# Chunk-wise copies at the end of two expert stages, and layer 1's combine weights in exchanged PSUM banks

## The reference, cut to what matters

```python
# layer 0: 64 experts, 8 chosen for each token, and a shared one
routed = sum over e of combine[:, e, None] * (relu2(xf @ up_w[e]) @ down_w[e])
x = x + gb * (routed + relu2(xf @ shared_up_w) @ shared_down_w)
# layer 1: 8 experts, all of them for each token
g = x @ w_gate[e];  u = x @ w_up[e];  h = silu(g) * u
cw = router_probs * gate_weights;  cw = cw / (sum(cw) + 1e-9)
x = x + gb * sum over e of cw[:, e, None] * (h @ w_down[e])
```

## Time and profile before

| what | us |
|---|---|
| time, median of 3 runs | 1149.88 (1149.51 to 1150.43) |
| the profiled execution | 1148.7 |
| its span, first to last instruction | 1147.0 |
| PE busy | 1071.9 (93%) |
| DVE busy | 897.1 (78%) |
| ACT busy | 746.7 (65%) |
| POOL busy | 247.2 (22%) |
| mean granted clock of PE | 0.982 of full |

### The profile page before, as it was taken

How to read it: one execution, slowest core, us unless ns; L and a number is a source line. 1 busy time by engine, 2 the same in 40 slices (tenths; PEclk the granted TensorE clock), 3 DMA queues, 4 the chain that set the end, 5 groups by cost and what they waited for, 6 DMA issues and landing times.

```text
span 1147.0 us, 18270 instructions
## 1 busy us (share of the span) xinstructions
PE 1071.9 (93%) x5699; PEld 595.5 (52%) x5699; DVE 897.1 (78%) x1786; ACT 746.7 (65%) x1098; POOL 247.2 (22%) x287
## 2 busy tenths in 40 slices
PE   7898888999999898899999999999979999999998
PEld 4333445777777432222222222223347888888886
DVE  6999985555654857999999999987547888887775
ACT  4885276888787234556667766787846666666664
POOL 0000005888889133311110011011110000000000
PEclk9999999999999998999999999999988999999999
DMA  6000017999982623310000000000002112101001
GB/s 184 1 0 1 1 51 161 217 221 223 205 181 57 144 53 65 59 49 2 2 2 1 2 2 2 1 2 1 2 1 103 65 65 65 47 22 61 0 1 37
DMA packets 40366, 67.63 MB, mean 59 GB/s; under 512 B 14810, under 2 KB 31354, under 8 KB 34810
## 3 DMA queue, kind: packets, MB, share of 16 engines
q1 hardware_dynamic: 40290, 66.61, 24.4%
HBM read 63.35 MB, written 3.11 MB: 58 GB/s over the span
## 4 chain that ended last, share of the span: by engine, by line
PE 60%; DVE 26%; ACT 5%; issue 5%; POOL 2%; DMA 1%; SPq 0%; POOLq 0%; DVEq 0%; ACTq 0%
PE ps L1067 10%; PE ps L1069 10%; PE ps L1068 10%; PE ps L1294 9%; DVE arena_b L2228 8%; PE ps L1230 7%; DVE arena_b L1931 3%; PE ps L1277 3%; PE ps L838 3%; POOL parts L777 2%; PE ps L1243 2%; DVE arena_b L2153 1%; ACT arena_b L1692 1%; DVE arena_b L2235 1%; ACT parts L1625 1%
## 5 line engine op out<-in xcount | busy, mean ns | idle before, releaser
L1692 ACT ACTIVATE arena_b<-ps 128x1024 f32<-128x1024 f32 (+3 forms) x320 | 272.8, 894 | 136.3 <-PE ps L1277 134.8
L1067 PE MATMUL ps<-parts 128*128 128x512 f32 x640 | 253.1, 395 | 11.2 <-POOL parts L777 8.7
L1069 PE MATMUL ps<-parts 128*128 128x512 f32 x640 | 250.0, 391 | 0.0
L1068 PE MATMUL ps<-parts 128*128 128x512 f32 x640 | 249.8, 390 | 0.0
L2228 DVE TENSOR_REDUCE arena_b<-ps 128x1 f32<-128x512 f32 x384 | 237.8, 681 | 7.1 <-PE ps L1230 5.8
L1230 PE MATMUL ps<-arena_a 48*128 48x128 bf16 (+5 forms) x832 | 185.0, 310 | 18.2 <-DVE arena_b L2228 9.6
L777 POOL TENSOR_TENSOR parts<-arena_b,parts 128x512 fp32r<-128x512 f32 x128 | 166.5, 1310 | 30.1 <-ACT parts L1625 25.3
L1230 PEld LDWEIGHTS ps<-arena_a 48*128 48x128 bf16 (+1 forms) x832 | 60.2, 94 | 204.6 <-DVE arena_b L2228 132.1
L1294 PE MATMUL ps<-arena_b 128*32 128x512 f32 (+3 forms) x1280 | 152.0, 547 | 1.1 <-POOL arena_b L821 0.6
L1067 PEld LDWEIGHTS ps<-parts 128*128 128x128 f32 x640 | 120.5, 188 | 48.3 <-POOL parts L777 20.2
L2153 DVE SCALAR_TENSOR_TENSOR arena_b<-ps,arena_a 128x512 f32<-128x512 f32 x128 | 86.9, 688 | 74.6 <-PE ps L1069 69.8
(11 more groups left out here) (311 smaller groups left out, 1104.5 us busy)
## 6 DMA issues: line engine op xcount, KB each, us to landing
arena_a<-root_weights SPq DMA_DIRECT2D x62, 512.0 KB, 8.9
arena_b<-expert_weights SPq DMA_DIRECT2D x7, 1024.0 KB, 6.3
arena_a<-q_parts SPq DMA_DIRECT2D x36, 64.0 KB
wslot<-in_L_ffn_up_w SPq DMA_DIRECT2D x8, 256.0 KB, 8.4
wslot<-in_L_ffn_down_w SPq DMA_DIRECT2D x8, 256.0 KB, 10.0
wslot<-in_L_ffn_w_gate SPq DMA_DIRECT2D x8, 256.0 KB, 2.7
wslot<-in_L_ffn_w_up SPq DMA_DIRECT2D x8, 256.0 KB, 3.0
wslot<-in_L_ffn_w_down SPq DMA_DIRECT2D x8, 256.0 KB, 3.8
```

Source lines behind the costliest of these rows:

```text
L1067: mm(bank, w(0), x(0), start=start, stop=False)
L1068: mm(bank, w(0), x(1), start=False, stop=False)
L1069: return mm(bank, w(1), x(0), start=False, stop=stop)
L1692: a(probs[:, s % 2, 2 * pair:2 * pair + 2, off:CW], ps[:, 2 + 2 * pair:4 + 2 * pair, off:CW], ACT.Exp, scale=scale).then_inc(p2_exp, 1)
```

## The change

Three edits. At the end of both expert stages ACT waits for each chunk's own last down product instead of for all of them. At the start of layer 1's expert stage the two sets of transposed weights change places (the broadcast one to banks 0 to 3, the 8-partition one to banks 4 to 7), and PE's wait for `cwT_ready` moves from before the first `look1` to the first `sum1` of each of banks 4 to 7. Six of the 20 spare matmuls before `cw_ready` are taken out.

```diff
             route1(NC - 1)
-            spare(20, 7)
+            spare(14, 7)
 
             pe.wait_ge(cw_ready, 1)
             for c in range(NC):
                 for k, t in enumerate(tiles(c)):
-                    last = mm(ps[:, 4 + c, k * P:(k + 1) * P], cw[:, t, 0:1].broadcast_to([P, P]), ident[:, :],
+                    last = mm(ps[:, c, k * P:(k + 1) * P], cw[:, t, 0:1].broadcast_to([P, P]), ident[:, :],
                               is_transpose=True, start=True, stop=True)
                 last.then_inc(cw_tr, 1)
             for t in range(NT):
-                last = nc.tensor.transpose(ps[0:E1, t // TPC, t % TPC * P:(t % TPC + 1) * P], cw[:, t, :],
+                last = nc.tensor.transpose(ps[0:E1, 4 + t // TPC, t % TPC * P:(t % TPC + 1) * P], cw[:, t, :],
                                            ident[:, :])
             last.then_inc(cw_tr, 1)
-            pe.wait_ge(cwT_ready, 1)
...
             def sum1(n0, k, first, last_one):
                 e, ft, c = k // (FT * NC), k // NC % FT, k % NC
+                if first:
+                    pe.wait_ge(cwT_ready, 1)
                 pe.wait_ge(ffn_lo, n0 + (k + 1))
...
             for c in range(NC):
-                if c == 0:
-                    act.wait_ge(moe_down, N_IT0 * MU)
+                act.wait_ge(moe_down, N_IT0 * MU - NC + c + 1)
                 a(yT[:, chunk(c)], ps[:, 4 + c, :], ACT.Copy, scale=modc[:, 0, 4:5]).then_inc(y0_ready, 1)
...
-            a(cwT[0:E1, :].rearrange("p (c t) -> p c t", c=NC), ps[0:E1, 0:4, :], ACT.Copy).then_inc(cwT_ready, 1)
+            a(cwT[0:E1, :].rearrange("p (c t) -> p c t", c=NC), ps[0:E1, 4:8, :], ACT.Copy).then_inc(cwT_ready, 1)
...
             for c in range(NC):
-                if c == 0:
-                    act.wait_ge(ffn_down, N_IT1 * MU)
+                act.wait_ge(ffn_down, N_IT1 * MU - NC + c + 1)
                 a(y1T[:, chunk(c)], ps[:, 4 + c, :], ACT.Copy, scale=modc[:, 1, 4:5]).then_inc(y1_ready, 1)
...
             for c in range(NC):
                 dve.wait_ge(cw_tr, c + 1)
-                v.tensor_tensor(hcf[:, c, :], ps[:, 4 + c, :], hT[:, PAD + c * CW:PAD + (c + 1) * CW], ALU.mult)\
+                v.tensor_tensor(hcf[:, c, :], ps[:, c, :], hT[:, PAD + c * CW:PAD + (c + 1) * CW], ALU.mult)\
                     .then_inc(hc_prod, 1)
```

## The result

The changed kernel takes 1148.0 us (median of 18 runs, 1142.82 to 1150.73) where the kernel before takes 1150.47 (18 runs, 1146.52 to 1155.48): a ratio of 0.9971, interval 0.9960 to 0.9982. By the ratio that is 3.3 us less (2.1 to 4.6 by the interval), by the two medians 2.5; forecast were 2.97. The profiled execution took 1145.96, with a span of 1144.2.

The account below looks back on a forecast made before the run. PE held 60% of the chain and DVE 26%, so gains had to come from hand-overs at the expert stages' rims. 0.95 + 1.05 + 0.97 = 2.97 us, from the median 1149.88, gave 1146.9 us; range 1144.9 to 1149.0.

Parts of the forecast that it names:

- Parts 1 and 4: Ends of layer 0's and layer 1's expert stages: chunk-wise copies let DVE's first addition start 0.95 and 0.97 us earlier.
- The rotary tables: Attention after layer 0: last table lands 9.5 us after issue, 3.9 us before first use, so the gain stays.
- Part 2: Start of layer 1's expert stage: six fewer spares let DVE's first product start 1.04 us earlier; bounds 0 and 1.24.
- full clock hides the spares: Before layer 1's combine weights: at full clock 20 spares end before the weights are ready, so cutting six gains 0.
- Part 3: Layer 1's first product: exchanging banks alone gains 0.03 us, because DVE's low parts end that close to the copy.
- The silu path: Layer 1's first units: table load and silu stay hidden with 0.2 us in hand, but would cap a larger gain.
- (c): Layer 1's start: the copy is the only gate, freeing its whole 1.87 us; 1146.7 at most, inside the forecast's 0.62.
- (b): Layer 1's start: spares held the clock; its fall loses 3.4 us against 2.97 gained, 1150.3 us; chance 0.07.
- (d): Before layer 1's weights: lower-clock stretches fall elsewhere, half of one goes, 1.7 us gained, 1145.2 us; chance 0.10.
- (a): Layer 0's end or the spares: one gain is lost to attention timing or full clock; 1147.9 us; chance 0.18.

Follow-up runs that it names:

- the changed kernel's third: The changed kernel, with nothing further altered, timed a third time against the kernel before: 1148.39 us, ratio 0.9969.

## Why the prediction was right

**Parts 1 and 4, the ends.** Forecast 0.95 and 0.97, measured 1.00 and 1.00, and the same to 0.01 us in every profile with the edit. It came out at the upper bound, 0.99: the transposes follow without a gap and the four take 0.45 us. By the rule of the Trainium skill that was cited ("TensorE: Matmul & The Clock Gate", "Part 2: What happens when you issue a matmul") it was 0.99, without it 0.92; the trace agrees with the rule. The rotary tables were the one step that came out otherwise: the prediction let the last one land 9.5 us after its issue as before, and it took 12.0, from 375.32 to 387.3, for a first use at 388.71. The 3.9 us in hand were 1.4. It was so in all ten profiles with early copies at layer 0's end (11.5 to 12.2 us, 1.2 to 1.9 in hand) and in none of the four without (9.3 to 10.9); why is not shown. The gain still came through whole: DVE took 11.15 us from its first addition to the last normalised chunk in both profiles.

**Part 2, the spares.** Forecast 1.04, measured 1.03 or 1.04 in all five executions with 14 spares before an idle stretch in which the weights end last. Its upper bound of 1.24 should read 1.26 (1.04 + 0.67 - 0.45), which changes nothing. The lower bound was put down to the wrong cause, though. It was drawn as "full clock hides the spares"; in none of the fourteen profiles was the clock full there, and what took the gain away was the clock being low later (6.48) and falling again (two of six). Over many executions the cut still pays: alone its ratio is 0.9982, interval 0.9970 to 0.9995. Beside the ends and the exchange it is not settled: 0.9977 with 20 spares against 0.9971, 0.9975 and 0.9969 with 14 is the right order, within overlapping intervals. Nor is it shown that the missing spares cause the falls: two of six against none of four can be chance. A link is possible, since the cut brings the idle stretch nearer to the clock's last rise, and the falls came where it was nearest.

**Part 3, the exchange.** Forecast 0.03, measured 0.01. The two gates stood 0.03 us apart, and the later one stayed. The silu path "would cap a larger gain", with 0.2 us in hand: with the first product 2.26 us earlier, the third unit came 0.24 earlier.

**The sum.** 2.97 forecast, 3.03 in the profile, 3.3 (2.1 to 4.6) by the times. The absolute 1146.9 is 1.1 under the 1148.0 measured. 0.6 of it come from the median it was set out from, 1149.88 over 3 runs and 1150.47 over 18; the other 0.5 lie within the spread of the runs.

**The rivals.** (c) is answered above. (b) and (d) did not come in the first profile: no fall behind the first product, and the stretch at 0.50 before the weights as long as before (861.5 to 868.3, for 862.2 to 869.1). (a)'s fear came true in another way: the attention did move, by -1.80, but by the clock and not by the change. The window 398 to 402 stood at 0.57 before and at 1.00 after; first before, then after:

```profile
398.00:402.00 4.00, 3.86 (x9) 1.94 (x9) 1.41 (x3) 1.21 (x2) 3.64 (x4) 0.57 0.41 105
```
```profile
398.00:402.00 4.00, 3.66 (x18) 2.09 (x18) 3.06 (x6) 1.36 (x2) 2.74 (x3) 1.00 0.35 84
```

A stretch at half clock that goes accounts for some 1.7 of the 1.80 (an estimate: 4.00 us at 0.57). With the same early copies at layer 0's end the stretch took 496.13 and 496.45 us in two other executions (the changed kernel's third and the one with 20 spares), so it is not the edit that shortens it. The +2.04 in front arose before the first expert stage (its first DVE product started at 183.0 instead of 181.0). Up to there all fourteen kernels are alike, and that start lay anywhere from 179.1 to 184.0; its cause was not looked for further.

## What to carry to other kernels

Where the profile names one releaser, look which other wait of the same instruction ends just before it: here the second ended 0.03 us before it, and taking the named one away alone gained 0.01. The second could then be cut too, and gained only together with the silu path behind it: 1.56 us for both, 0.24 or nothing for one. At the end of an accumulation over several banks, let the copy of each bank wait for its own last product: the hand-over behind the last one then shows neither a copy nor idle time of PE, 1.00 us less here. And read a change of 0.3% stretch by stretch between fixed instructions; the whole time of one execution spreads by more than it.

## What was not expected of the hardware

PE's granted clock makes a large part of the spread: the stretch from layer 0's first addition to layer 1's weights took from 494.66 to 500.70 us with the same work, with the clock at 0.52 or 0.83 of full in the same ten us of it. It does not explain all: what lies before that stretch ended anywhere from 370.5 to 374.8 us, for reasons not looked for. After 2.0 us of idle PE went on at full clock in eight of ten executions and fell to 1.2 GHz within 1 us of the first product in two. And with no filler at all, PE stayed at 1.2 GHz for 13 us, from 863 to 876, first busy, then 4.64 us idle, then busy with the transposes.
